# First attention: row sums from the value products, brought to the values' rows by permutation products, the quotient on GpSimd, the output product one sequence later

## What is computed

```python
def _L0_attn_ref(x, w_in, w_out):
    qkv = jnp.einsum('bse,fe->bsf', x, w_in)
    q, k, v = jnp.split(qkv, 3, axis=-1)
    o = _sliding_window_attention(heads(q), heads(k), heads(v), WIN)   # WIN = 64
    ...
    return jnp.einsum('bse,fe->bsf', o, w_out)

def _sliding_window_attention(q, k, v, win):
    ...
    scores = jnp.einsum('bhnqd,bhnkd->bhnqk', qb, k2) * scale
    scores = jnp.where(valid, scores + bias, -jnp.inf)
    p = jax.nn.softmax(scores, axis=-1)
    out = jnp.einsum('bhnqk,bhnkd->bhnqd', p, v2)
```

## Time and profile before

| | |
|---|---|
| three timed runs | 1714.79, 1716.84, 1717.81 us |
| their median | 1716.84 us |
| span of the profiled execution | 1708.8 us |
| busy over the span: PE, DVE, ACT, POOL | 1513.5, 1319.0, 1217.6, 1099.4 us |

### The profile page before, as it was taken

One profiled execution on the slowest core, in us unless ns is written; L12 is line 12 of the kernel. 1 busy time (PEld: TensorE's weight loads), 2 busy tenths in 40 slices (PEclk: granted clock), 3 DMA queues, 4 the chain that ended last, 5 costly groups with the idle time before them and its releaser, 6 DMA issues. The chain is left out here.

```text
span 1708.8 us, 44008 instructions
## 1 busy us (share of the span) xinstructions
PE 1513.5 (89%) x16988; PEld 1164.6 (68%) x16988; DVE 1319.0 (77%) x2187; ACT 1217.6 (71%) x2065; POOL 1099.4 (64%) x661
## 2 busy tenths in 40 slices
PE   5899996999999499999999578899999999999885
PEld 4677774677776266666666467777777777777774
DVE  5899974555655699999997788887888888888753
ACT  2677774545445488888888378888888888888873
POOL 1777752555555388888887477776676777667614
PEclk8899998999999699999999689999999999999997
DMA  5000000000000500000000001111111110111113
GB/s 174 2 3 3 3 3 15 15 8 7 7 7 1 185 2 2 14 2 14 2 14 11 13 22 31 27 26 27 27 27 27 27 26 22 26 27 27 27 27 105
DMA packets 56837, 44.12 MB, mean 26 GB/s; under 512 B 28152, under 2 KB 47900, under 8 KB 56388
## 3 DMA queue, kind: packets, MB, share of 16 engines
q1 hardware_dynamic: 56644, 41.45, 9.1%
HBM read 17.75 MB, written 4.23 MB: 13 GB/s over the span
## 5 line engine op out<-in xcount | busy, mean ns | idle before, releaser
L831 POOL TENSOR_TENSOR a_prob<-a_prob,a_top 128x1024 f32<-128x1024 f32 x128 | 239.8, 1895 | 48.2 <-DVE a_top L1023 48.2
L1237 POOL TENSOR_TENSOR e_hh<-e_h,e_hh 128x512 fp32r<-128x512 f32 x112 | 144.8, 1293 | 146.6 <-ACT e_hh L1221 145.2
L1506 POOL TENSOR_TENSOR i_qk<-i_qk,i_rt 128x1024 f32<-128x1024 f32 x64 | 152.0, 2375 | 38.1 <-DVE i_rt L1955 33.3
L1516 POOL TENSOR_TENSOR i_qk<-i_qk,i_rn 128x1024 f32<-128x1024 f32 x64 | 122.5, 1915 | 80.5 <-DVE i_rn L1934 80.5
L1019 DVE TENSOR_TENSOR a_prob<-ps,a_table 128x1024 f32<-128x1024 f32 x128 | 149.7, 1211 | 23.4 <-PE ps L899 21.3
L1811 ACT ACTIVATE i_prob<-i_prob,i_top 128x128 f32<-128x128 f32 x512 | 156.4, 391 | 15.7 <-DVE i_top L1943 13.8
L977 ACT ACTIVATE a_probT<-ps 128x1024 f32<-128x1024 f32 x128 | 131.3, 1026 | 44.5 <-PE ps L907 44.5
L1258 DVE TENSOR_TENSOR e_h<-ps,e_sg 128x512 f32<-128x512 f32 x112 | 77.3, 690 | 104.3 <-PE ps L1120 90.4
L907 PEld LDWEIGHTS ps<-ident,a_prob 128*128 128x128 f32 x1024 | 113.2, 141 | 64.2 <-ACT a_probT L977 50.3
L1503 POOL TENSOR_TENSOR i_qk<-i_raw,i_rot 128x1024 f32<-128x1024 f32 x59 | 140.3, 2378 | 24.1 <-issue 24.1
L1208 ACT ACTIVATE e_sg<-ps 128x512 f32<-128x512 f32 x112 | 67.0, 598 | 123.2 <-PE ps L1120 122.4
(11 more groups left out here) (305 smaller groups left out, 4369.3 us busy)
## 6 DMA issues: line engine op xcount, KB each, us to landing
i_V<-i_V SPq DMA_DIRECT2D x96, 130.0 KB, 2.3
a_table<-skew_scratch SPq DMA_DIRECT2D x2, 2048.0 KB, 12.4
X<-in_L_attn_x SPq DMA_DIRECT2D x4, 512.0 KB, 6.1
a_table<-in_c_l_table SPq DMA_DIRECT2D x1, 2048.0 KB, 8.3
e_xs<-Y SPq DMA_DIRECT2D x8, 256.0 KB, 2.3
i_ms<-Y SPq DMA_DIRECT2D x16, 128.0 KB, 2.4
i_ms<-Y SPq DMA_DIRECT2D x16, 112.0 KB, 2.4
out_dram<-X SPq DMA_DIRECT2D x7, 256.0 KB, 2.3
```

The source lines that it names most:

```text
L831: nc.gpsimd.tensor_tensor(s, s, top[:, slot].unsqueeze(2).broadcast_to([P, HG, KW]), ALU.subtract).then_inc(shifted, 1)
L1237: nc.gpsimd.tensor_tensor(hh[0:n, slot(b, parity), 1, :], h[0:n, slot(b, parity), :], hh[0:n, slot(b, parity), 0, :].bitcast(F32), ALU.sub ...
L1506: nc.gpsimd.tensor_tensor(s, s, rt[:], ALU.add).then_inc(rotated, 1)
L1516: nc.gpsimd.tensor_tensor(flat, flat, rn[:, T // TPB % 2, T % TPB].unsqueeze(2).broadcast_to([P, 2 * FH, FD]), ALU.mult).then_inc(qk_done, 1)
```

## The change

The values' tile V has 40 places for four heads of eight features. The change writes ones into free places of it, so that the value products leave values and row sums in bank 6 together: the heads with even x in the left 128 columns and those with odd x in the right 128, each with its sums on the rows of the neighbouring head. The ones products are dropped. ScalarE copies both halves into `both` (`keep_sums`). In a new job `d` of each sequence, at step 7 of its count, TensorE multiplies with permutation tiles (`pick`) so that the sums of both tiles come to the values' rows, in bank 7. VectorE takes the reciprocal of 128x256 (`denominators`), which frees the bank; GpSimd makes the quotients (`scale`), one of 128x256 for each tile. The output product takes two matrices `wO`, one for each half, and comes at the `xy` job five sequences later instead of four. In `front` one semaphore takes the place of two.

```diff
@@ window_attention, GpSimd
-            nc.gpsimd.memset(ones[:], 0.0)
-            nc.gpsimd.memset(V[:], 0.0).then_inc(zeroed, 1)
+            nc.gpsimd.memset(V[:], 0.0)
             pool.drain()
-            for x in range(QG):
-                nc.gpsimd.memset(ones[:, x, 0:D], 1.0).then_inc(zeroed, 1)
+            flat = V[:].rearrange('p b v k g x d -> p (b v k g) x d')
+            for at in (D, 4 * D):
+                nc.gpsimd.memset(flat[:, :, 0:QG:2, at:at + D], 1.0).then_inc(zeroed, 1)
...
+            def scale(i):
+                pool.wait_ge(aux_free, job_of('d', i))
+                for k in range(TPB):
+                    after(pool, aux_ps, job_of('xy', i - 2 + DELAY) if i >= 2 else 0)
+                    nc.gpsimd.tensor_tensor(oT[:, i % 2, k], both[:, i % 2, k], den[:, i % 2, k].unsqueeze(1).broadcast_to([P, 2, P]),
+                                            ALU.mult).then_inc(o_sb, 1)
...
             for n in range(UNITS):
...
+                i, r = divmod(n - 14, U)
+                if r == 0 and i >= 0:
+                    scale(i)
                 shift(n)
@@ window_attention, steps of the jobs
-        AT = {'xy': -7, 'qk': -6, 'v': 0}
+        AT = {'xy': -7, 'qk': -6, 'v': 0, 'd': 7}
-        DELAY = 4
+        DELAY = 5
@@ window_attention, TensorE
-                            last = nc.tensor.matmul(ps[:, 7, (2 + k) * P:(3 + k) * P], oT[:, T % 4, :], wT[:, 3, :], start=True, stop=True)
+                            for w in range(2):
+                                last = nc.tensor.matmul(ps[:, 7, (2 + k) * P:(3 + k) * P], oT[:, (i - DELAY) % 2, k, w, :], wO[:, w, :], start=w == 0, stop=w == 1)
+                elif kind == 'd':
+                    pe.wait_ge(biased, 1)
+                    for k in range(TPB):
+                        pe.wait_ge(both_sb, i * TPB + k + 1)
+                        for w in range(2):
+                            last = nc.tensor.matmul(ps[:, 7, k * P:(k + 1) * P], pick[:, w, :], both[:, par, k, w, :], start=w == 0, stop=w == 1)
...
-                        for g in range(4):
-                            src = probT[:, (2 * m + g // 2) % 4]
-                            at = ((g % 2 * XX + xx) * KT + k) * P
-                            last = nc.tensor.matmul(ps[32 * g:32 * g + 32, 6, P:2 * P], ones[:].rearrange('p x d -> p (x d)')[:, 32 * x:32 * x + 32], src[:, at:at + P], start=False, stop=final and k == KT - 1, tile_position=(0, 32 * g))
@@ window_attention, ScalarE, ahead of the exponential of every second step
+            def keep_sums(T):
+                act.wait_ge(pv, (T + 1) * NU)
+                after(act, o_sb, T - 3)
+                nc.scalar.activation(both[:, T // TPB % 2, T % TPB].rearrange('p w q -> p (w q)'), ps[:, 6, 0:2 * P], ACT.Copy).then_inc(both_sb, 1)
@@ window_attention, VectorE
-                nc.vector.reciprocal(rden[:, :], ps[:, 6, P:2 * P])
-                dve.drain()
-                nc.vector.tensor_tensor(oT[:, T % 4, :], ps[:, 6, 0:P], rden[:, :], ALU.mult).then_inc(o_sb, 1)
+            def denominators(n, i):
+                dve.wait_ge(aux_ps, n + 1)
+                after(dve, o_sb, TPB * (i - 1))
+                nc.vector.reciprocal(den[:, i % 2].rearrange('p k q -> p (k q)'), ps[:, 7, 0:TPB * P]).then_inc(aux_free, 1)
```

More of the change, by code:

```diff
@@ L495, in window_attention @@
         V = sb('V', [P, 2, NVT, TPB, 4, QG, 40])
-        ones = sb('ones', [P, QG, 40])
         prob = sb('prob', [P, NBUF, HG, KW])
@@ L499, in window_attention @@
         probT = sb('probT', [P, 4, 1024])
[L500 to L503, removed]
+        both = sb('both', [P, 2, TPB, 2, P])
+        den = sb('den', [P, 2, TPB, P])
+        oT = sb('oT', [P, 2, TPB, 2, P])
+        pick = sb('pick', [P, 2, P])
+        wO = sb('wO', [P, 2, P])
+        parity = sb('parity', [P, 2])
+        zeroed, aux_ps, aux_free, k_sb, masked, scores, biased, max_done, shifted, exped, p_T, pT_sb, pv, both_sb, o_sb = map(sem, ('zeroed', 'aux_ps', 'aux_free', 'k_sb', 'masked', 'scores', 'biased', 'max_done', 'shifted', 'exped', 'p_T', 'pT_sb', 'pv', 'both_sb', 'o_sb'))
         block = c.enter_context(nc.Block())
         NBL = 32
-        NZERO = 5 + 2
-        AT = {'xy': -7, 'qk': -6, 'v': 0}
+        NZERO = 4
+        AT = {'xy': -7, 'qk': -6, 'v': 0, 'd': 7}
         FIRST = AT['xy']
-        DELAY = 4
+        DELAY = 5
         LAST = (NBATCH + DELAY - 1) * U + AT['xy'] + 1
@@ L562, in _ @@
                     mask_keys(i)
+                i, r = divmod(n - 14, U)
+                if r == 0 and i >= 0:
+                    scale(i)
                 shift(n)
-                i, r = divmod(n + 2, U)
+            for i in range((UNITS - 14 + U - 1) // U, NBATCH):
+                scale(i)
         @block.tensor
@@ L615, in sums @@
                 if pair == 0 and part == 0:
-                    after(pe, o_sb, i * TPB + tile)
+                    after(pe, both_sb, i * TPB + tile)
                     pe.wait_ge(aux_free, job_of('v', i))
@@ L628, in sums @@
                                 cols = slice(WIN * w, WIN * (w + 1))
-                                nc.tensor.matmul(ps[32 * g:32 * g + 32, 6, cols], vals[:, 32 * x:32 * x + 32], src[:, at + cols.start:at + cols.stop], start=first and k == 0 and (cols.start == 0), stop=False, tile_position=(0, 32 * g))
-                        for g in range(4):
-                            src = probT[:, (2 * m + g // 2) % 4]
-                            at = ((g % 2 * XX + xx) * KT + k) * P
-                            last = nc.tensor.matmul(ps[32 * g:32 * g + 32, 6, P:2 * P], ones[:].rearrange('p x d -> p (x d)')[:, 32 * x:32 * x + 32], src[:, at:at + P], start=False, stop=final and k == KT - 1, tile_position=(0, 32 * g))
+                                out = slice(P * (x % 2) + cols.start, P * (x % 2) + cols.stop)
+                                last = nc.tensor.matmul(ps[32 * g:32 * g + 32, 6, out], vals[:, 32 * x:32 * x + 32], src[:, at + cols.start:at + cols.stop], start=first and w == 0, stop=final and w == 1, tile_position=(0, 32 * g))
                 last.then_inc(pv, 1)
@@ L682, in _ @@
             for step in range(FIRST, LAST):
+                T, at = divmod(step, NU)
+                if at == 0 and 2 <= T < TILES + 2:
+                    keep_sums(T - 2)
                 if 0 <= step + 1 < UNITS:
@@ L685, in _ @@
                 for n, kind, i in jobs_at(step):
-                    job(n, kind, i)
+                    if kind != 'd':
+                        job(n, kind, i)
                 if 0 <= step < UNITS:
@@ L705, in row_max, with output_weights @@
                 nc.vector.tensor_reduce(top[:, slot], prob[:, slot], AX.X, ALU.max).then_inc(max_done, 1)
-            def normalise(T):
-                dve.wait_ge(pv, (T + 1) * NU)
-                after(dve, aux_ps, job_of('xy', T // TPB - 2 + DELAY) if T >= 4 else 0)
-                nc.vector.reciprocal(rden[:, :], ps[:, 6, P:2 * P])
-                dve.drain()
-                nc.vector.tensor_tensor(oT[:, T % 4, :], ps[:, 6, 0:P], rden[:, :], ALU.mult).then_inc(o_sb, 1)
-            def job(n, kind, i):
+            def output_weights():
+                blocks = ident[:, :].rearrange('p (a b j) -> p a b j', b=2, j=D)
+                picked = pick[:].rearrange('p w (a b j) -> p w a b j', b=2, j=D)
+                nc.vector.memset(pick[:], 0.0)
+                nc.vector.tensor_tensor(parity[:, :], own[:, 0:2], own[:, 2:4], ALU.add)
+                dve.drain()
+                for w in range(2):
+                    nc.vector.tensor_copy(picked[:, w, :, w, :], blocks[:, :, 1 - w, :])
+                for w in range(2):
+                    nc.vector.tensor_scalar_mul(wO[:, w, :], wT[:, 3, :], parity[:, w:w + 1])
+                dve.drain()
+            def denominators(n, i):
                 dve.wait_ge(aux_ps, n + 1)
[L716 to L719, removed]
+                after(dve, o_sb, TPB * (i - 1))
+                nc.vector.reciprocal(den[:, i % 2].rearrange('p k q -> p (k q)'), ps[:, 7, 0:TPB * P]).then_inc(aux_free, 1)
+            output_weights()
             for step in range(FIRST, LAST):
-                T, r = divmod(step - 1, NU)
                 n = step + AHEAD
-                if r == 0 and 1 <= T <= TILES:
-                    normalise(T - 1)
+                for a, kind, i in jobs_at(step - 1):
+                    if kind == 'd':
+                        denominators(a, i)
                 if step % 2 == 0 and 0 <= n < UNITS:
```

16 lines of the change are left out of this document (5 added, 11 removed).

## The result

The changed kernel takes 1724.22 us (median of 4 runs, 1722.37 to 1727.61), the kernel before 1715.82 (4 runs, 1712.67 to 1717.81). The ratio is 1.0056, with a 95% interval of 1.0036 to 1.0077: slower by 6 to 13 us. The forecast was 1720.7, that is 3.9 us slower.

What follows compares the result with a forecast made beforehand. TensorE was taken to set the first attention's pace, 12.95 us a sequence, and afterwards the loop through VectorE's reciprocal, 12.83. Terms −1.3 + 0.6 + 4.6 = +3.9 us on 1716.84 gave 1720.7 us, range 1716.5 to 1725.5.

Steps and rivals of the forecast that it cites:

- the loop: First attention: scores, VectorE's additions and maxima, reciprocal, `v`, back to scores; 12.83 us, setting the period instead of TensorE.
- rival of slower value products: In `sums`, weight loads hold adjacent value groups: 0.30 us instead of 0.24 each; +6.9 us, 1723.7; chance 0.15.
- 12.19 of the forecast: TensorE's own work per attention sequence after the change, in us: 12.95 − 0.36 − 1.72 + 0.88 + 0.44.
- The start: Before the first mask, GpSimd gets two longer fills and loses clearing and four small fills: +0.6 us.
- a floor: In `sums`, value products keep a 27 ns floor whatever their columns: +13.9 us, 1730.7; chance 0.04.
- hidden reciprocal: The 128x256 reciprocal costs 1.1 us or less, so TensorE's 12.19 us sets the period: −4.5 us, 1712.3; chance 0.10.
- the one through ScalarE: ScalarE's copy waiting for GpSimd's quotient uses up 3.4 us of cover; 1 us beyond costs 11 us, 1731.7; chance 0.05.
- Routing sequences, counted at 0: First four attention sequences, with routing work: VectorE is slowest there before as after, so no gain or loss counted.
- The end, +4.6: Last sequence: `v` waits for the reciprocal, 2.3 us later, and the chain after the last transposes grows 2.3 us.
- Steady loop, −1.3: From the fifth attention sequence on, 11 periods each gain 0.12 us, from 12.95 to 12.83.
- The fill, counted at 0: First four attention sequences fill the stage, with VectorE slowest before as after; nothing counted for them.
- 8.0 us lie around the span: Outside the profiled span: median 1716.84 us against a span of 1708.8, a difference the change doesn't touch.

Runs made afterwards that it cites:

- e2: Changed kernel with VectorE's reciprocal of the row sums placed between the two maxima of the pair before it; 1.0028 of the kernel before.
- e4: Changed kernel with the reciprocal of only one tile per sequence (128x128 instead of 128x256), the other tile's quotient left out; 1.0032 of the kernel before.
- e1b: Kernel before with only the front's two semaphores merged into one, timed a second time; 0.9996 of the kernel before.
- e8: Changed kernel with VectorE's routing work cut in seven pieces instead of five, nothing else; 1720.29 us, 1.0031 of the kernel before.
- e9: Kernel before with its routing work cut in the same seven pieces, without the change; 0.9989 of the kernel before.
- e3: Changed kernel with five spare 128x256 products ahead of the value projection at three long waits for the reciprocal; 1725.02 us, 1.0087 of the kernel before.

## Why the prediction was right, and where its steps failed

The direction and the loop held. The time did so in part by luck: 1724.22 lies above the 1718 to 1723.5 that the forecast gives to its own mechanism, and inside 1716.5 to 1725.5 only because that range takes in the rival of slower value products, which did not happen. The forecast's 3.9 us also lie below the 6 to 13 us measured. The period is 12.82 (12.83 forecast), the reciprocal 1.75 (1.76), a call of `sums` 0.58 (202.50 to 203.08; 0.59), and `v` waits for the reciprocal; e2 and e4 show that without this the period goes to 12.42. TensorE's own period is thus 0.23 above the 12.19 of the forecast, and the wait 0.33 instead of 0.64. The forecast took off 0.36 us of rest, which is the idle time in the row of the weight loads; TensorE's products rested only 0.10 us (12.85 busy of 12.95), and with that the same sum gives 12.45. The start is +0.59 (+0.6). The rivals of slower value products and of a floor fell with the call; for the first, "nothing in the trace shows two value groups in a row" had overlooked the second attention, where 32 value products of 128 columns follow each other in 1.01 us (700.96 to 701.97 in the trace of before). The one of a hidden reciprocal fell too, and so did the one through ScalarE: in the quiet sequence its copy waits 0.55 us for GpSimd, and no product waits for it.

The size did not hold. Against the mean of the four profiles with the attention of before (230.78, 228.96, 229.86 and e1b's 229.28: 229.7) the attention is 11.1 us longer, against 3.9 forecast:
- **Routing sequences, counted at 0** ("the routing work makes VectorE the slowest there, before as after"): +6.2 us, masks 3 to 6. This is the step that failed. Before, VectorE was the slowest (13.77 busy of 14.07 us), and TensorE waited 1.22 us in the first of these sequences, for the quotient, and kept its clock. Afterwards VectorE is not the slowest (14.31 of 17.93): the reciprocal that `v` waits for stands behind the routing piece and the additions and maxima, so TensorE idles 1.22 us ahead of the scores and 2.80 us ahead of `v`; then it runs at 1.2 GHz. e8 shows that short pieces take all of it away (38.77 us; 38.84 in e9); e3 puts at least 2.6 us on the clock. The stretch of L272 from 0.43 to 2.13 us is argued to be part of the rest: e8 shortened the stretch and the pieces together.
- **The end, +4.6** (its two parts, 2.27 and 2.24, add up to 4.5): measured +6.5 from the last scores. Both waits came as worked out: last scores to `v` 7.55 us (7.56), last transposes to the end 11.03 (10.9). But from `v` to the last transposes it is 9.89 us instead of 8.06: after the wait of 2.28 us `v`, transposes and products together are 1.6 us slower, at a lower clock. "The shorter products are used up" missed that.
- **Steady loop, −1.3:** from mask 6 on only −0.4 (−0.23 to mask 15, −0.13 to the last scores), since two of those sequences take 13.29 us: the rounding of routing weights (1.09 to 1.64 us) delays the reciprocal there as well.
- **The fill, counted at 0:** −1.2 us, mean 35.1 in the five profiles with the attention's order of before (e9 among them) and 33.9 in the eight with the changed one; in the one profile of the changed kernel −1.8, which is what the 11.1 holds. 0.9 of it repeats in every profile: masks 2 to 3 take 12.5 us in the five and 11.6 in the eight. Here too VectorE was not the slowest: TensorE was busy for 12.39 of these 12.49 us before, and for 10.88 of 11.58 after. The rows, before and changed:

```profile
60.08:72.57 12.49, 12.39 (x273) 9.09 (x272) 11.53 (x15) 9.70 (x16) 9.36 (x5) 1.00 0.01 3
63.63:75.21 11.58, 10.88 (x209) 7.76 (x208) 10.09 (x12) 10.12 (x18) 9.36 (x6) 1.00 0.01 2
```

The forecast is 3.5 us below the result: its difference was too small by 4.5 (8.4 between the medians) and its base too high by 1.0. "8.0 us lie around the span" was wrong: in every later run the time is 1.8 to 2.2 us above the span. The first profile, with a span of 1708.8, was a quick execution, and it was compared with a slower median.

Open: the timed differences of the eight kernels with the changed order (the ratio less one, times 1714) lie on average 2.5 us above what their attention shows against 229.7 (e2 and e3 most), while starts and rests of their profiles don't differ from those of before beyond scatter (starts 29.3 to 37.0 against 30.8 to 38.2, rests 1448.0 to 1451.9 against 1447.2 to 1450.6).

## What to carry to other kernels

When a change ties two engines together at a new place, work out its wait in every sequence, above all in those where other work stands in the queue ahead of the one waited for. A wait on a tight engine is paid twice if the clock falls after it. If work must sit in a critical queue, cut it to pieces that fit the idle time there.

## What was not expected of the hardware

- TensorE's granted clock fell to 1.2 GHz in the middle of a busy stage: after idling 1.22 and, one group of scores later, 2.80 us, `v` took 2.08 instead of 1.16 and the transposes 1.91 instead of 1.04. It fell likewise after 1.22 and 1.67 us (e2), after 1.22 and 2.00 us (e4), and in the second routing sequence of the changed kernel after 1.76 us alone (transposes 1.92). It stayed at full speed where spare products filled the wait (e3).
- 32 value products of 64 columns in a row took 0.65 us with their drain; taking away the ones products between them did not slow them down (a call of `sums` 0.58 us; 0.59 by the value products' rows of before).
- One 128x256 operation of VectorE with both inputs in SBUF took 0.43 us, or up to 2.13 beside a GpSimd pass.
